# Attention with a random draw: the draw of two batches made at once, in 32 columns

## The reference

```python
sb, rb = 10, 50
cam = (kidx < sb) | (kidx >= T - rb)
scores = where(cam, Q K^T / sqrt(32), neg);  probs = softmax(scores, -1)
e = T - rb; ws = e + 1                      # 50 and 51
last = probs[..., -1, :]                    # the last query's row, per batch and head
mean_attn = last[..., ws:].mean(-1) + 1e-06
p = clip(last[..., e] / mean_attn, 0.0, 1.0)
mask = (bern_u < p)                         # bern_u: 16 given numbers, one per head
v_e = V[..., e, :] * mask[..., None] / rb
V = V.at[..., ws:end, :].add(v_e)           # keys 51 to 99
out = probs @ V;  out = out.transpose(...).reshape(B, T, D) @ wo.T
```

## Time and profile before

| | us |
|---|---|
| median of 3 runs | 3014.05 |
| lowest and highest | 3012.68 and 3017.73 |
| the profiled execution, its own time | 3016.01 |
| its span, first to last instruction | 3014.1 |
| mean granted clock of TensorE | 0.969 of full |
| VectorE busy over the span | 1517.1 |
| ScalarE busy over the span | 978.0 |

### The profile page before, as it was taken

The page is one execution under the profiler, slowest core; times in us unless marked ns, Lnnn a source line. Parts: engine busy times, 40 slices in busy tenths (PEclk is TensorE's granted clock), DMA queues, the critical chain, the costliest instruction groups (busy, mean ns, idle before and its releaser), DMA issues.

```text
span 3014.1 us, 37838 instructions
## 1 busy us (share of the span) xinstructions
PE 2809.8 (93%) x14808; PEld 1777.9 (59%) x14808; DVE 1517.1 (50%) x2855; ACT 978.0 (32%) x2540; POOL 683.2 (23%) x676
## 2 busy tenths in 40 slices
PE   8999989998999999999998999999988988878888
PEld 4555555555756656687554555555555656666666
DVE  4545655766555566311467667665477661111115
ACT  2320341204443333221462322332144433333331
POOL 0150113500200000242023222110000226656640
PEclk9999999999799999999999999999999989999999
DMA  4110121100011011585000011011001037754447
GB/s 175 42 56 21 57 99 42 46 9 1 33 67 36 28 39 46 200 318 171 24 32 15 13 36 37 27 46 43 21 29 53 33 95 247 251 188 155 142 150 185
DMA packets 66677, 249.12 MB, mean 83 GB/s; under 512 B 26554, under 2 KB 28602, under 8 KB 53764
## 3 DMA queue, kind: packets, MB, share of 16 engines
q1 hardware_dynamic: 31776, 177.88, 17.5%
q0 software_dynamic: 31344, 65.30, 6.6%
q10 hardware_dynamic: 3380, 3.53, 0.4%
HBM read 274.53 MB, written 42.13 MB: 105 GB/s over the span
## 4 chain that ended last, share of the span: by engine, by line
PE 74%; DVE 13%; ACT 5%; another core or an unknown queue 3%; issue 2%; DMA 2%; POOL 1%; SPq 0%; ACTq 0%; POOLq 0%; DVEq 0%
PE P L1089 19%; PE P L1556 10%; PE P L1093 10%; PE P L1206 5%; PE P L1442 4%; PE P L1099 4%; PE P L1424 4%; PE P L1164 2%; PE P L1165 2%; PE P L1101 1%; PE P L1118 1%; ACT A L1722 1%; PE P L1415 1%; DVE A L2350 1%
## 5 line engine op out<-in xcount | busy, mean ns | idle before, releaser
L1616 ACT ACTIVATE A<-P 128x400 f32<-128x400 f32 (+4 forms) x589 | 302.2, 530 | 566.3 <-PE P L1442 170.9
L2626 DVE TENSOR_TENSOR A<-P,A 128x128 f32<-128x128 f32 (+1 forms) x141 | 44.9, 318 | 554.7 <-ACT A L1905 492.1
L1089 PE MATMUL P<-A,W 128*128 128x400 f32 x840 | 312.4, 509 | 5.4 <-DVE A L2274 2.9
L1089 PE MATMUL P<-X,W 128*128 128x400 f32 x816 | 305.0, 511 | 11.6 <-DMA W<-weights 8.8
L1089 PEld LDWEIGHTS P<-A,W 128*128 128x128 f32 x840 | 159.6, 193 | 126.4 <-issue 9.0
L1089 PEld LDWEIGHTS P<-X,W 128*128 128x128 f32 x816 | 154.7, 193 | 129.6 <-issue 16.2
L1099 PE MATMUL P<-C,A 128*128 128x128 f32 (+5 forms) x1463 | 205.3, 263 | 15.2 <-DVE A L2240 6.4
L1099 PEld LDWEIGHTS P<-C,A 128*128 128x128 f32 (+5 forms) x1463 | 166.9, 145 | 62.5 <-issue 44.5
L2757 POOL DMA_INDIRECT A<-tokens,A x141 | 144.5, 1025 | 195.5 <-issue 76.9
L1816 ACT ACTIVATE A<-P,small 100x361 f32<-100x361 f32 x256 | 142.6, 561 | 140.7 <-DVE small L2359 140.7
L1556 PE MATMUL P<-A 128*128 128x128 f32 x1280 | 159.2, 283 | 23.9 <-ACT A L1616 22.0
(11 more groups left out here) (378 smaller groups left out, 5089.6 us busy)
## 6 DMA issues: line engine op xcount, KB each, us to landing
W<-weights SPq DMA_DIRECT2D x60, 1024.0 KB, 4.8
A<-experts SPq DMA_DIRECT2D x16, 1536.0 KB
W<-experts SPq DMA_DIRECT2D x28, 768.0 KB
KT<-experts SPq DMA_DIRECT2D x15, 768.0 KB
W<-weights SPq DMA_DIRECT2D x17, 640.0 KB, 3.9
A<-experts SPq DMA_DIRECT2D x14, 768.0 KB
A<-outputs SPq DMA_DIRECT2D x12, 768.0 KB
W<-outputs SPq DMA_DIRECT2D x8, 768.0 KB
```

What stands on the lines that cost most here:

```text
L1089: self.e.matmul(out, a, b, start=i == 0, stop=False)
L1616: self.e.activation(out, in_, ACT.Copy).then_inc(*self.of(*item))
```

## The change

Three groups of operands that each batch had for itself are laid out for a pair. `c.EF` is the pair's weights seen as 32 rows (head, then batch) of 64 columns; `c.field(k, p)` is one of six groups of 32 columns for pair p, and `c.of_batch(k, b)` the 16 of them that belong to one batch, which are every second one. The maximum and the sums of one batch are written to and read from those.

Inverse sums, draw, shares and last key's addition are left out for an even batch and made for both in the odd one's step, on twice the columns. The pair's first instruction waits for both batches' exponentials. The matmul that spreads the mask and the two instructions of `last_key` are made once for a pair as well, and the transposes wait for one event instead of two. Only sub-layer 9 has this path.

```diff
+        c.EF = [E.rearrange("p h a k -> p (h a) k")[0:S] for E in c.EP]
+        c.field = lambda k, p: self.small[0:S, 192 * (p % 3) + 32 * k:192 * (p % 3) + 32 * k + 32]
+        c.of_batch = lambda k, b: c.field(k, b // 2).rearrange("p (h a) -> p h a", a=2)[:, :, b % 2]
...
     def last_key(self, c, b):                       # TensorE
+        if b % 2 == 0:
+            return
         P = self.take(("plan", "last", b), ("vadd", b))
         self.wait_ge(self.at("bern", b))
-        self.e.matmul(P[0:S, 0:16], self.c["lastrow"][0:S, :], c.M[b % 6][0:S, 48:64],
+        self.e.matmul(P[0:S, 0:32], self.c["lastrow"][0:S, :], c.field(3, b // 2),
...
-            self.wait_ge(self.at("shares", c.n, b - 1))
             self.wait_ge(self.at("shares", c.n, b))
...
+        if c.special:                               # ScalarE, exps
+            top, total = c.of_batch(0, b), c.of_batch(1, b)
+            for h in range(16):
+                i = self.e.activation(e[0:S, h, :], e[0:S, h, :], ACT.Exp, scale=scale, bias=top[:, h:h + 1], accum_out=total[:, h:h + 1])
+            i.then_inc(*self.of("exps", c.n, b))
+            return
...
+        if c.special:                               # VectorE, shares
+            return self.pair_shares(c, b) if b % 2 else None
...
+    def pair_shares(self, c, b):
+        e, w = c.EF[b // 2 % 3], c.field(5, b // 2)
+        self.wait_ge(self.at("exps", c.n, b - 1))
+        self.wait_ge(self.at("exps", c.n, b))
+        self.e.reciprocal(w, c.field(1, b // 2)).then_inc(*self.of("inverse", "heads", c.n, b))
         self.wait_ge(self.at("inverse", "heads", c.n, b))
-        if c.special:
-            self.bernoulli(c, b, e, m)
-        v = e[0:S, :, 0:c.nk]
-        self.e.tensor_tensor(v, v, bc(m[0:S, 80:96], [S, 16, c.nk], 2), ALU.mult).then_inc(
+        self.bernoulli(c, b, e)
+        v = e[:, :, 0:c.nk]
+        self.e.tensor_tensor(v, v, bc(w, [S, 32, c.nk], 2), ALU.mult).then_inc(*self.of("bern_step", 7, b))
...
-        self.e.tensor_tensor(a, self.c["bern"][0:S, :], a, ALU.is_lt).then_inc(*self.of("bern", b))
+        a = a.rearrange("p (h a) -> p h a", a=2)
+        self.e.tensor_tensor(a, bc(self.c["bern"][0:S, :], [S, 16, 2], 2), a, ALU.is_lt).then_inc(*self.of("bern", b))
...
     def last_key(self, c, b):                       # VectorE
-        e, m = c.E[b % len(c.E)], c.M[b % 6]
-        edge, r, u = e[0:S, :, c.SB], m[0:S, 32:48], m[0:S, 64:80]
+        if b % 2 == 0:
+            return
+        edge, r, u = c.EF[b // 2 % 3][:, :, c.SB], c.field(2, b // 2), c.field(4, b // 2)
```

More of the change, by code:

```diff
@@ L2186, in scores @@
             i.then_inc(*self.of("masked", c.n, b, g))
+        top = c.of_batch(0, b) if c.special else m[0:S, 0:16]
         self.wait_ge(self.at("masked", c.n, b, 3))
-        self.e.tensor_reduce(m[0:S, 0:16], e[0:S, :, 0:c.nk], AX.X, ALU.max, negate=True).then_inc(*self.of("top", c.n, b))
+        self.e.tensor_reduce(top, e[0:S, :, 0:c.nk], AX.X, ALU.max, negate=True).then_inc(*self.of("top", c.n, b))
         if c.late:
@@ L2192, in scores @@
         scale = float(np.float32(1.0) / np.sqrt(np.float32(32)))
-        self.e.tensor_scalar(m[0:S, 0:16], m[0:S, 0:16], scale, None, ALU.mult).then_inc(*self.of("max", c.n, b))
+        self.e.tensor_scalar(top, top, scale, None, ALU.mult).then_inc(*self.of("max", c.n, b))
     def shares(self, c, b):
+        if c.special:
+            return self.pair_shares(c, b) if b % 2 else None
         e, m = c.E[b % len(c.E)], c.M[b % 6]
@@ L2200, in shares, with bernoulli @@
         self.e.reciprocal(m[0:S, 80:96], m[0:S, 16:32]).then_inc(*self.of("inverse", "heads", c.n, b))
-        if not c.special:
-            return
-        self.wait_ge(self.at("inverse", "heads", c.n, b))
-        if c.special:
-            self.bernoulli(c, b, e, m)
-        v = e[0:S, :, 0:c.nk]
-        self.e.tensor_tensor(v, v, bc(m[0:S, 80:96], [S, 16, c.nk], 2), ALU.mult).then_inc(
-            *self.of("bern_step", 7, b) if c.special else self.of("shares", c.n, b))
-    def bernoulli(self, c, b, e, m):
-        a, r, w, u = (m[0:S, i:i + 16] for i in (48, 32, 80, 64))
+    def pair_shares(self, c, b):
[3 more added lines that the diff above has]
+        self.e.reciprocal(w, c.field(1, b // 2)).then_inc(*self.of("inverse", "heads", c.n, b))
+        self.wait_ge(self.at("inverse", "heads", c.n, b))
+        self.bernoulli(c, b, e)
+        v = e[:, :, 0:c.nk]
+        self.e.tensor_tensor(v, v, bc(w, [S, 32, c.nk], 2), ALU.mult).then_inc(*self.of("bern_step", 7, b))
+    def bernoulli(self, c, b, e):
+        r, a, u, w = (c.field(k, b // 2) for k in range(2, 6))
         mark = lambda n: self.of("bern_step", n, b)
         after = lambda n: self.wait_ge(self.at("bern_step", n, b))
-        self.e.tensor_reduce(r, e[0:S, :, c.SB + 1:c.NK], AX.X, ALU.add).then_inc(*mark(0))
+        self.e.tensor_reduce(r, e[:, :, c.SB + 1:c.NK], AX.X, ALU.add).then_inc(*mark(0))
         after(0)
@@ L2224, in bernoulli @@
         after(4)
-        self.e.tensor_tensor(a, a, e[0:S, :, c.SB], ALU.mult).then_inc(*mark(5))
+        self.e.tensor_tensor(a, a, e[:, :, c.SB], ALU.mult).then_inc(*mark(5))
         after(5)
@@ L2228, in bernoulli @@
         after(6)
-        self.e.tensor_tensor(a, self.c["bern"][0:S, :], a, ALU.is_lt).then_inc(*self.of("bern", b))
+        a = a.rearrange("p (h a) -> p h a", a=2)
+        self.e.tensor_tensor(a, bc(self.c["bern"][0:S, :], [S, 16, 2], 2), a, ALU.is_lt).then_inc(*self.of("bern", b))
     def last_key(self, c, b):
-        e, m = c.E[b % len(c.E)], c.M[b % 6]
-        edge, r, u = e[0:S, :, c.SB], m[0:S, 32:48], m[0:S, 64:80]
+        if b % 2 == 0:
+            return
+        edge, r, u = c.EF[b // 2 % 3][:, :, c.SB], c.field(2, b // 2), c.field(4, b // 2)
         self.wait_ge(self.at("plan", "last", b))
-        self.e.scalar_tensor_tensor(out=r, in0=self.ps("plan", "last", b)[0:S, 0:16], scalar=1.0 / 50, in1=u, op0=ALU.mult,
+        self.e.scalar_tensor_tensor(out=r, in0=self.ps("plan", "last", b)[0:S, 0:32], scalar=1.0 / 50, in1=u, op0=ALU.mult,
                                     op1=ALU.mult).then_inc(*self.of("vadd", b))
```

## The result

| | before | changed |
|---|---|---|
| median of 11 runs, us | 3014.05 | 3025.09 |
| lowest and highest | 3008.70, 3020.65 | 3017.66, 3030.55 |
| ratio changed to before | | 1.0034, 95% interval 1.0021 to 1.0046 |
| span of the profiled execution | 3014.1 | 3023.2 |
| VectorE busy, instructions | 1517.1, 2855 | 1510.9, 2807 |

The ratio is +10.2 us (6 to 14) on 3014; the medians lie 11.0 apart, and the two profiled executions 9.1 (3016.01 and 3025.09). 3022.8 was forecast. VectorE has 48 instructions and 6.2 us of work less, and the kernel takes longer.

A forecast was written before the change was run, and what follows sets the result against it. VectorE was taken to lead in the stage before; after merging, a ring through the odd batch's exponentials binds. Ring 5.9 plus low TensorE clock 2.8 gave +8.7 on 3014.05, so 3022.8 us; range 3013.5 to 3028, own range 3020.3 to 3025.

The forecast's parts named there:

- (a): VectorE before: one batch's inverse, draw and shares 3.78 us; scores' copies, maximum and scaling 2.65; last key 0.30.
- (b): VectorE's merged chain on 32 columns: 5.88 us a pair by slopes, bounds 3.78 and 7.56.
- (c): VectorE's own work: 1.98 us less per pair, 7.9 us over four pairs, 48 instructions gone.
- (d): Added wait for the odd batch's exponentials closes a cycle of 16.44 us against 15.45, +0.99 per pair.
- The ring: Cycle of exponentials, pair's shares, next scores, last key, transposes, ScalarE copies, next exponentials: 16.44 us per pair.
- (e): Sum along the last key's additions: batch 1 +1.80, 3 and 5 +0.99 each, 7 +2.10; total +5.88 us.
- (f): TensorE's longer idle stretches lower its clock at the transposes and the stage's end: +2.8 us.
- (g): Behind the stage: the delay passes through whole, summing to +8.7 us.
- (1): Rival: VectorE sets the pace and merging pays, 3008.9 or 3006.2 us; chance 0.08.
- (2): Rival: the cycle through the exponentials binds but the clock costs nothing, +5.9, 3019.9 us; chance 0.20.
- (3): Rival: TensorE's clock is low nearly throughout, +11, 3025 us; chance 0.10.
- (4): Rival: merged addressing or something behind the stage takes the delay away, +0 to +3, 3014 to 3017 us; chance 0.07.

The follow-up runs named there:

- e3: Changed kernel with the pair's inverse, draw and shares made in two 16-column chains, both behind the odd batch's exponentials; ratio to before 1.0060, stage 116.16 us.
- e1: Changed kernel with filler matmuls on TensorE around the last key's matmuls; ratio to before 1.0015, stage 103.37 us.
- e2: Changed kernel with the last key's addition ahead of the next odd batch's scores in steps 5 and 7; ratio to before 1.0021, stage 102.62 us.
- e4: Changed kernel, each batch keeping its own inverse, sum and multiplication, only the draw's small operations and last key per pair; ratio to before 0.9991, stage 94.87 us.

## Why the prediction was right, step by step

(a), (b) The pair's chain was put at 5.88 us and takes 5.91; reduction, multiplication and reciprocal were put at 1.79, 2.15 and 0.342 and take 1.786, 2.152 and 0.353. Slopes from two lengths of the same operation carried twice the length. The formula of the Trainium skill ("VectorE: DVE Perf Modes", section on the TRN2 errata) gave 2157 ns for the multiplication; the trace agrees with it, at 2152. The rearranged addresses cost nothing that shows: the maximum, which now writes every second column, takes 1.153 us as before, one exponential 0.332 against 0.331.

(c) VectorE's busy time fell by 6.2 us, all of it in the stage, where 7.9 were worked out. The 7.9 go from start to start and hold some 0.035 us of waiting between an instruction and the next one that depends on it (in e3's chain 2254.69 to 2254.97 for a reciprocal of 0.25); nine of the twelve instructions saved in a pair had such a gap, 36 in all or some 1.3 us, which busy time leaves out, and the pair's parts came out some 0.06 us dearer. So the sign "7.6 to 8 us less busy time" was missed for the way it was counted, not for the work.

(d) The ring of 16.44 us: 16.60 and 16.63 with the clock held (e1), of which 7.83 and 7.85 from the addition to the inverse (7.71 forecast) and 8.77 and 8.78 from there (8.73). e2 and e3 shorten and lengthen it and the distances follow. The 2 to 4 us of idle time ahead of the inverse were 1.6 to 2.0; another 1.6 us stand ahead of the even batch's copies of scores, which wait for TensorE. (e) Batch 1 +1.80: measured +1.82. In all, the clock aside, 5.88 were forecast. e1's stage is 4.70 longer than before, and before had paid 1.65 for a fall of the clock at and behind its last transposes (12.78 against 11.13), so the ring cost 6.35: 1.78 at batch 1, 1.15 and 1.17 for the next two, 2.25 at batch 7.

(f) The size that was off is the clock, put at +2.8. Changed against e1: 0.40, 1.28, 1.11 and 2.55, 5.3 us; less the 1.65 that the kernel before paid, 3.7. I had taken 0.60 us a group at the low clock from the earlier trace rows, which had caught only one distance in a set that was half through; whole sets run at 0.67, so each costs 1.3 and not 1.0. The miss is nearly all in batches 3 and 5: I had put the first distance at 0.5 and the next two together at 1.5, and they cost 0.4 and 2.4, since both sets ran low throughout, where I had counted three quarters of the price; the end was put at 0.8 and cost 0.9. TensorE's waits ahead of the transposes, put at some 8 us, are 3.9 to 5.7 long. The rule of the Trainium skill ("TensorE: Matmul & The Clock Gate", Part 1) that idleness halves the clock holds here, by 0.50 at these transposes and by 0.66 against 0.80 in the middle. By stages the sum is 6.35 + 3.7 = 10.1 us, the whole difference of the stages (108.75 - 98.67) and, within its interval, of the total.

(g) The delay passed through, to within 1 us: stage +10.1, total +10.2 by the ratio. In the two profiled executions the stage begins 1.6 us earlier and ends 8.5 later, and the span is 9.1 longer.

Of the rivals, (1) needed the inverse to start without waiting, and it waits; (2) is e1, a kernel with fillers, not this one; (4) is out. (3) is nearer in its sum, 3025, than the forecast's 3022.8: it had 5.1 us for the clock and the forecast 2.8, and 3.7 were measured, with a clock that is 0.66 and not low throughout. Both parts of the forecast came out low, 6.35 against 5.9 and 3.7 against 2.8, so the number owes nothing to errors that cancel. In the chances "half of (2)" would be 0.10 where 0.08 is written.

## What to carry to other kernels

Before merging two instances of a step into one larger instruction, find what the second instance waits for. The first one's work may have been done inside that wait, for nothing; merged, it stands behind it. Merge what is short, where twice the columns cost little more (an operation of the draw takes 0.17 us on 16 columns and 0.18 on 32), leave what is long by itself (the multiplication takes 1.15 and 2.15 us; e4), and look at how far ahead the awaited engine was: here 1.11 us of slack against 2.1 us of added length.

## What the runs showed of the hardware that I had not expected

The low clock cost time here although TensorE was busy for only 73% of the middle: sets of 16 small transposes lie in the chain between two other engines, and three of the four run at 0.67 us a group instead of 0.35. That and the low clock behind the last set cost 5.3 us, and 27 filler matmuls in TensorE's idle time gave it back (e1). Two chips differed by 3.3% on the same program (3019.25 and 2919.89 us before, 29 and 33 runs), and the parts of this stage that can be compared are equally long on both; times on one say nothing about the other, ratios on one chip do.
